# Attention pass of a four-layer graph network: each block of edges is summed by one flat scan over feature-major rows in PSUM instead of a tree of row-by-row multiply-adds

## The reference

```python
h = (x @ W_node).reshape(n, H, HD)                   # H = 4 heads of HD = 16
attn = a_src_node[src] + a_dst_node[dst] + edge_attr @ W_edge
attn = jnp.where(attn >= 0, attn, NEG_SLOPE * attn)
attn_max = jnp.zeros((n, H), attn.dtype).at[dst].max(attn)
attn = jnp.exp(attn - attn_max[dst])
attn_sum = jnp.zeros((n, H), attn.dtype).at[dst].add(attn)
attn = attn / (attn_sum[dst] + EPS_SOFTMAX)
msg = h[src] * attn[:, :, None]
out = jnp.zeros((n, H, HD), h.dtype).at[dst].add(msg).reshape(n, OUT_DIM)
y = out + h.reshape(n, OUT_DIM)                      # then a layernorm with gamma and beta
```

## Time and profile before

| what | value |
| --- | --- |
| time, median of 3 runs | 11177.78 us (11177.54 to 11199.18) |
| span of the profiled execution | 11181.7 us |
| profiled instructions | 57120 |
| DVE busy, whole span | 4736.9 us |
| ACT busy, whole span | 1142.1 us |
| POOL busy, whole span | 7106.9 us |
| attention pass, first gather to the end of the last | 8707.2 to 10967.1 us |

### The profile page before, as it was taken

The page is one execution under the profiler, slowest core; times in us unless marked ns, Lnnn a source line. Parts: engine busy times, 40 slices in busy tenths (PEclk is TensorE's granted clock), DMA queues, the critical chain, the costliest instruction groups (busy, mean ns, idle before and its releaser), DMA issues.

```text
span 11181.7 us, 57120 instructions
## 1 busy us (share of the span) xinstructions
PE 1801.6 (16%) x9285; PEld 1516.5 (14%) x9285; DVE 4736.9 (42%) x20005; ACT 1142.1 (10%) x2728; POOL 7106.9 (64%) x6884
## 2 busy tenths in 40 slices
PE   8744444444000400000000000000001000000000
PEld 7633333333000300000000000000000000000000
DVE  8855555555797422222221222222224344444446
ACT  0143434343000100000000000000000000000000
POOL 0566666666201377777776677777777776666766
PEclk7755555555555555555555555555555555555555
DMA  5144444444575111111111111111111222222221
GB/s 224 57 129 122 129 124 126 124 127 122 204 273 203 32 50 46 48 46 48 46 48 37 50 46 48 46 48 46 48 46 30 54 53 58 53 58 55 56 55 44
DMA packets 570444, 911.29 MB, mean 81 GB/s; under 512 B 333435, under 2 KB 348228, under 8 KB 544824
## 3 DMA queue, kind: packets, MB, share of 16 engines
q1 hardware_dynamic: 350264, 652.74, 17.3%
q0 software_dynamic: 219904, 255.88, 10.8%
HBM read 494.12 MB, written 414.02 MB: 81 GB/s over the span
## 4 chain that ended last, share of the span: by engine, by line
DVE 34%; issue 28%; another core or an unknown queue 17%; POOL 16%; PE 3%; DMA 1%; ACT 1%; DVEq 0%; SPq 0%; POOLq 0%; ACTq 0%
DVE arena_a L1495 16%; POOL arena_a L641 15%; DVE arena_b L1112 4%; DVE arena_a L1110 3%; DVE arena_b L1125 3%; DVE arena_a L1425 3%; POOL arena_a L610 2%; PE bank L811 2%; DVE arena_b L1056 1%; DVE arena_b L1093 1%; PE bank L916 1%; DVE arena_a L1625 0%; PE bank L890 0%; DMA arena_a<-in_a 0%
## 5 line engine op out<-in xcount | busy, mean ns | idle before, releaser
L641 POOL DMA_INDIRECT arena_a<-table_c,decay x3136 | 3284.6, 1047 | 1257.6 <-issue 1051.2
L1495 DVE SCALAR_TENSOR_TENSOR arena_a<-arena_a,same_dst 128x64 f32<-128x64 f32 x3134 | 891.5, 284 | 3449.5 <-DVE arena_a L1495 2713.2
L591 POOL DMA_INDIRECT by_src<-arena_b,idx_blk x1568 | 1570.8, 1002 | 885.8 <-issue 449.4
L641 POOL DMA_INDIRECT arena_a<-table_at,decay x1568 | 1556.8, 993 | 703.8 <-issue 468.4
L1110 DVE SCALAR_TENSOR_TENSOR arena_a<-arena_a,same_dst 128x64 f32<-128x64 f32 x1567 | 441.9, 282 | 711.1 <-remote 547.7
L864 PE MATMUL bank<-ident,chunk_end 128*64 128x128 f32 (+2 forms) x8 | 2.7, 442 | 4416.0 <-DVEq L973 4416.0
L864 PEld LDWEIGHTS bank<-ident,chunk_end 128*64 128x64 f32 (+2 forms) x8 | 1.4, 240 | 4416.6 <-DVEq L973 4416.6
L1112 DVE SCALAR_TENSOR_TENSOR arena_b<-arena_a,src_f,before 128x128 bf16<-128x128 f32 x1568 | 543.7, 347 | 37.4 <-issue 37.4
L850 PE MATMUL bank<-hrows 98*128 98x128 f32 x1568 | 404.0, 440 | 659.5 <-DVE arena_b L1125 331.9
L850 PE MATMUL bank<-hrows,arena_a 98*128 98x128 f32 x1568 | 403.3, 438 | 658.0 <-DVE arena_b L1125 347.4
L753 ACT ACTIVATE arena_b<-arena_a,decay 128x64 f32<-128x64 f32 x1568 | 394.2, 334 | 972.5 <-remote 610.2
(11 more groups left out here) (279 smaller groups left out, 4845.9 us busy)
## 6 DMA issues: line engine op xcount, KB each, us to landing
arena_a<-ids_rows SPq DMA_DIRECT2D x98, 1024.0 KB
states_src<-arena_a SPq DMA_DIRECT2D x98, 1024.0 KB
states_c<-arena_a SPq DMA_DIRECT2D x196, 512.0 KB
hrows<-by_src SPq DMA_DIRECT2D x98, 776.0 KB, 6.1
states_at<-arena_a SPq DMA_DIRECT2D x98, 576.0 KB
x_at_start<-arena_a SPq DMA_DIRECT2D x7, 7168.0 KB, 49.0
arena_a<-x_at_start SPq DMA_DIRECT2D x98, 512.0 KB
arena_a<-table_c,decay POOLq DMA_INDIRECT x3136
```

The costliest lines, as they stand in the source:

```text
L591: pool.indirect_dma_start(out=by_src, out_offset=AT(ap=idx_blk[r][:, k:k + 1], axis=0), in_=rows[r][:, k, :], in_offset=None)\
L641: pool.indirect_dma_start(out=gb[r][:, k * w:(k + 1) * w], out_offset=None, in_=table[g], in_offset=AT(ap=src_i[:, n * J + k:n * J + k + 1 ...
L1495: ins = v.scalar_tensor_tensor(out=st[h][:, k * D:(k + 1) * D], in0=old, scalar=same_dst[:, e:e + 1], in1=gb[r][:, k * D:(k + 1) * D], op0 ...
```

## The change

In the attention pass the tree of 33 operations goes. The rows to be summed now lie feature by feature: for each of the 68 columns, 17 slots of which slot 0 holds the carried sum and slots 1 to 16 the block's edges. That is 1156 elements per partition. A single scan `new = mask * old + in` over them makes all sums of the block; the mask is 0 in slot 0 of each column, so that one column does not run into the next. The input of the scan (`in0`) lies in PSUM, over three of its eight banks, and so do the exponentials (`p_ex`). DVE's weighing writes into `in0` directly, turned from edge-major to feature-major. ACT gets two new operations per block: `mask_spread` copies 16 mask values into all 68 columns, and `rows_back` turns the finished sums into the edge-major rows that SP stores, and raises `state`. POOL reuses a row buffer once the block in it is weighed (`weighed`). Before, it had to be summed. The score steps now stand in two groups, steps 0 to 2 ahead of the scan and 3 to 6 behind it. PE's two outputs move to other banks, the tables of products and their 14 operations go, and two memsets of the masks come in ahead of the first convolution. The convolutions keep their chain.

```diff
-                               ("ex", HEADS * (J + 1)), ("msk0", HEADS * (J + 1) + 1),
-                               ("msk1", HEADS * (J + 1) + 1), ("tmp", W3)])
+                               ("sums0", W3 * (J + 1)), ("sums1", W3 * (J + 1))])
...
+        by_feature = carve(arena_b[:, KN * W01 - 2 * W3 * (J + 1):], [(f"mask{h}", W3 * (J + 1)) for h in range(2)])
+        by_feature.update((name, late[name]) for name in ("sums0", "sums1"))
...
+        banks = ps("banks", [P, 8 * 512])
+        bank = [banks[:, n * 512:(n + 1) * 512] for n in range(8)]
+        by_feature.update((f"in{h}", banks[:, h * 3 * 512:(h + 1) * 3 * 512]) for h in range(2))
...
-        p_turned = [bank[1 + h][:, 0:J * E16] for h in range(2)]
-        p_score = [bank[3 + h][:, 0:J * HEADS] for h in range(2)]
+        p_turned = [bank[3 + h][:, 0:J * E16] for h in range(2)]
+        p_score = [bank[5 + h][:, 0:J * HEADS] for h in range(2)]
+        p_ex = bank[7][:, 0:HEADS * (J + 1)]
...
                 for n in range(NBLK):
-                    if n >= R:
+                    if n >= R and g == "at":
+                        pool.wait_ge(s("weighed"), n - R + 1)
+                    elif n >= R:
                         pool.wait_ge(s("state"), upto(g, "state") + n - R + 1)
...
+        def mask_spread(act, g, n):
+            w = W3 if g == "at" else D
+            if n >= 2:
+                act.wait_ge(s("summed"), upto(g, "summed") + n - 1)
+            act.activation(features(f"mask{n % 2}", w)[:, :, 1:J + 1], bf(same_dst[:, n * J:(n + 1) * J], w), ACT.Copy)\
+               .then_inc(s("mask_spread"), 1)
+        def rows_back(act, g, n):
+            w, row = (W3, W3S) if g == "at" else (D, D)
+            act.wait_ge(s("summed"), upto(g, "summed") + n + 1)
+            if n >= 2:
+                act.wait_ge(s(f"stored{n % 2}"), upto(g, f"stored{n % 2}") + 16 * (n // 2))
+            act.activation(st[n % 2][:, 0:J * row].rearrange("p (j f) -> p j f", f=row)[:, :, 0:w],
+                           features(f"sums{n % 2}", w)[:, :, 1:J + 1].rearrange("p f j -> p j f"), ACT.Copy)\
+               .then_inc(s("state"), 1)
...
                 act.wait_ge(s("at_args"), n + 1)
-                act.activation(late["ex"], late["df"], ACT.Exp).then_inc(s("at_exp"), 1)
-                g3 = gb[n % R].rearrange("p (j w) -> p j w", w=W3)
-                act.activation(by_head(g3)[:, :, :, HD], slots("df")[:, :, 1:J + 1].rearrange("p c j -> p j c"),
-                               ACT.Exp).then_inc(s("at_exp"), 1)
+                act.activation(p_ex, late["df"], ACT.Exp).then_inc(s("at_exp"), 1)
+                act.activation(weighed(n)[:, :, HD, 1:J + 1], slots("df")[:, :, 1:J + 1], ACT.Exp).then_inc(s("at_exp"), 1)
+                if n:
+                    rows_back(act, "at", n - 1)
+            rows_back(act, "at", NBLK - 1)
...
-            def sums_of(n, raw, carried, made, scored=None):
...
-                carried = chunk_end[:, 0:W3] if n == 0 else st[1 - h][:, (J - 1) * W3S:(J - 1) * W3S + W3]
                 if n:
-                    v.wait_ge(s("state"), upto("at", "state") + n)
-                v.tensor_tensor(late["tmp"].rearrange("p (c d) -> p c d", d=HS),
-                                carried.rearrange("p (c d) -> p c d", d=HS),
+                    v.wait_ge(s("summed"), upto("at", "summed") + n)
+                    carried = weighed(n - 1, "sums")[:, :, :, J]
+                else:
+                    carried = chunk_end[:, 0:W3].rearrange("p (c d) -> p c d", d=HS)
+                v.tensor_tensor(weighed(n)[:, :, :, 0], carried,
                                 slots("ex")[:, :, 0:1].to_broadcast([P, HEADS, HS]), ALU.mult)
-                hview = by_head(g3)[:, :, :, 0:HD]
-                v.tensor_tensor(hview, hview, ex_e.rearrange("p j (c o) -> p j c o", o=1)
+                v.tensor_tensor(weighed(n)[:, :, 0:HD, 1:J + 1].rearrange("p c d j -> p j c d"),
+                                by_head(g3)[:, :, :, 0:HD], ex_e.rearrange("p j (c o) -> p j c o", o=1)
                                 .to_broadcast([P, J, HEADS, HD]), ALU.mult).then_inc(s("weighed"), 1)
                 if ahead:
-                    score_step(n + 1, 0)
+                    for step in range(3):
+                        score_step(n + 1, step)
                 v.wait_ge(s("weighed"), n + 1)
-                sums_of(n, g3, late["tmp"], s3[:, :, 0:W3], n + 1 if ahead else None)
+                if n >= 2:
+                    v.wait_ge(s("state"), upto("at", "state") + n - 1)
+                v.tensor_tensor_scan(by_feature[f"sums{h}"], by_feature[f"mask{h}"],
+                                     by_feature["in0"][:, 0:W3 * (J + 1)], 0.0, ALU.mult, ALU.add).then_inc(s("summed"), 1)
+                if ahead:
+                    for step in range(3, 7):
+                        score_step(n + 1, step)
```

More of the change, by code:

```diff
@@ L55 @@
     "table_out": 16 * len(PARTS),
-    "onehots": 2 * NB, "onehots_used": 2 * NB, "flag": 1, "flagrow": 1, "chain": (J - 1) * NBLK,
+    "onehots": 2 * NB, "onehots_used": 2 * NB, "flag": 1, "flagrow": 1, "chain": (J - 1) * NBLK, "mask_spread": NBLK, "summed": NBLK,
 }
@@ L61 @@
                            CONVS))
+ORDER.update(dict.fromkeys(("mask_spread", "summed"), ("at",)))
 ORDER.update(dict.fromkeys(("onehots", "onehots_used"), ("dst", "src")))
@@ L347, in slots, with weighed @@
         def slots(name):
-            return late[name].rearrange("p (c j) -> p c j", j=J + 1)
+            return (p_ex if name == "ex" else late[name]).rearrange("p (c j) -> p c j", j=J + 1)
+        def weighed(n, name="in0"):
+            return features(name if name == "in0" else f"{name}{n % 2}", W3).rearrange("p (c d) j -> p c d j", d=HS)
         def rows_of(dram_ap, w):
@@ L357, in scattered, with features @@
             return s(f"scattered{n % R}"), n // R * (16 * J)
+        def features(name, w):
+            return by_feature[name][:, 0:w * (J + 1)].rearrange("p (f j) -> p f j", j=J + 1)
         def blk(i, h):
@@ L677, in dense_act @@
                 turned_act(act, g, p, i)
+        def mask_spread(act, g, n):
[12 more added lines that the diff above has]
+               .then_inc(s("state"), 1)
         def attention_act(act):
-            def mask_of(n):
-                act.activation(msk[n % 2][:, 0:HEADS * (J + 1)].rearrange("p (c j) -> p c j", j=J + 1)[:, :, 1:J + 1],
-                               bf(same_dst[:, n * J:(n + 1) * J], HEADS), ACT.Copy).then_inc(s("at_mask"), 1)
             def edges_turned(n):
@@ L691, in attention_act @@
             act.wait_ge(s("at_begun"), 1)
-            mask_of(0)
+            mask_spread(act, "at", 0)
             edges_turned(0)
@@ L1521, in conv_nodes @@
                 link(v.tensor_tensor(rows3, rows3, per_node(dinv, p, D), ALU.mult))
-            for span, product in run.items():
-                uppers = same_dst[:, :].rearrange("p (m two k) -> p m two k", two=2, k=span)[:, :, 1, :]
-                to = product.rearrange("p n (m k) -> p (n m) k", k=span)
-                link(v.tensor_copy(to, uppers))
-                for k in range(1, span):
-                    link(v.tensor_tensor(to[:, :, k], to[:, :, k], to[:, :, k - 1], ALU.mult))
+            for h in range(2):
+                link(v.memset(by_feature[f"mask{h}"], 0.0))
             conv("c1")
@@ L1565, in _ @@
             link(v.memset(late["mx"], 0.0))
-            for h in range(2):
-                link(v.memset(msk[h], 0.0))
             tell("at_begun")
@@ L1595, in score_step @@
                     v.wait_ge(s("score"), n * 5 + 3)
-                    v.wait_ge(s("at_mask"), n + 1)
-                    v.tensor_tensor_scan(late["fw"], msk[h][:, 0:slot_count], late["lk"], 0.0, ALU.mult, ALU.max)\
+                    v.wait_ge(s("mask_spread"), upto("at", "mask_spread") + n + 1)
+                    v.tensor_tensor_scan(late["fw"], by_feature[f"mask{h}"][:, 0:slot_count], late["lk"], 0.0, ALU.mult, ALU.max)\
                         .then_inc(s("score"), 1)
@@ L1600, in score_step @@
                     v.wait_ge(s("score"), n * 5 + 4)
-                    v.tensor_tensor_scan(late["mx"][:, ::-1], msk[h][:, 1:slot_count + 1][:, ::-1],
+                    v.tensor_tensor_scan(late["mx"][:, ::-1], by_feature[f"mask{h}"][:, 1:slot_count + 1][:, ::-1],
                                          late["fw"][:, ::-1], 0.0, ALU.mult, ALU.max).then_inc(s("score"), 1)
```

55 lines of the change are left out of this document (1 added, 54 removed).

## The result

The changed kernel takes 11108.16 us (median of 4 runs, 11103.21 to 11112.4), against 11185.37 us for the kernel before (median of 4 runs, 11177.54 to 11199.18). The ratio is 0.9926, with a 95% interval of 0.9912 to 0.994: faster by 0.7%. A second set, 5 runs against 9 on one chip, gives 0.9928 (0.9915 to 0.9942). The direction was forecast. The size was not: 290 us were expected, and 77 came.

The account below looks back on a forecast made before the run. POOL's gathers, delayed by a late DVE, were taken as the bound. Gathers 1950.6 plus 9.2 plus 15 make 1975 us instead of 2259.9, minus 285, with the tail minus 290: 10888 us, range 10868 to 10990.

Parts of the forecast that it names:

- The floor of POOL: Attention pass: a gather takes 0.944 us plus 0.30 before the next, so sixteen need at least 19.9 us per block.
- POOL's waits: Attention pass: POOL's waits for DVE's tree or a missing releaser go once buffers are free after weighing, minus 235.4 us.
- Count, not length: Attention pass: while POOL gathers, DVE gets one instruction per 1.3 to 1.4 us, so 43 need 57 us, 11 need 14.7.
- Stretch: Attention pass: DVE lengthens gathers by 76.6 us; 9.2 from four scans stay, 15 us are left for the rest.
- Prices: Attention blocks: scan 2.61 us, weighing 1.22, mask and copy of rows about 1.10 each, all hidden behind POOL's 19.9.
- the tail: Start of the last attention gather to first copy after the pass: 12.3 us instead of 17.0, 4.7 less.
- B: Rival, attention pass: DVE's instructions still come too slowly, fifteen at 1.40 us, 21.0 us per block; 10980 us, chance 0.15.
- D: Rival, attention pass: slow DVE instructions plus scan and weighing not overlapping, 24.8 us per block; slower, 11343 us, chance 0.05.
- E: Rival, attention pass: POOL's pauses have another cause than a late DVE and stay; nothing happens, 11178 us, chance 0.05.
- C: Rival, attention pass: scan and weighing hold gathers despite PSUM input, 2.3 us per block, 225 us; 11113 us, chance 0.05.

## Why the prediction was wrong, step by step

- **The floor of POOL, "sixteen of them make 19.9 us, the least that POOL needs for a block".** This is the step that failed. 19.98 us holds up to the eleventh block, then 22.40 (22.43 with the full kernel) is the least. The term "1568 x (0.944 + 0.30) = 1950.6" should have been that of the gathers alone, 2173.6 us, which has the four scans at its start in it. From 2260.3 that leaves 87 us to be had, and the change took 81. With 2173.6 in the place of 1975 the sum would have given some 11086 us, where 11108 was measured. The trace of before held the figure: both convolutions end in blocks of 22.40 us. In the first one, 9 blocks from the second on and 10 later are (length, POOL's busy time):

```profile
3870.20:4050.10 179.90, 136.02 (x144) 0.50 0.20 50
5167.40:5391.40 224.00, 169.72 (x161) 0.50 0.18 47
```

  I read that as DVE's chain, whose instructions come 1.40 us apart; it was POOL's, since with three DVE instructions per block in place of the chain these passes keep their length.
- **POOL's waits, -235.4 us.** They went, all of them. The price was wrong: a pause of POOL is given back as fast gathers (16.2 us for 16.2 in the run with one pause). By that run, the pauses of the kernel before had kept its gathers fast, so the limit did not show in this pass: its quickest blocks take 19.96 to 20.1 us from its start to its end.
- **Count, not length.** Right in kind: 43 instructions without length rebuild the old pass. As a fixed 1.33 us per instruction it is wrong, as 19 instructions show. The rows of before could have told: 4149 DVE instructions in 2259.9 us are one per 0.54 us, and 43 at 1.33 would need 57 us of a block of 23.06. Behind this: "Runtime: NRT & Kernel Launch" of the Trainium skill, section "Instruction fetch mechanics", has fetching mostly hidden. One-element copies 1.40 us apart are not bound by their work. In the pass with 43 instructions per block the queue that carries instructions moved 53 blocks of 8192 bytes, in 0.3 to 0.8 us each. That is few and short beside some 450 steps of 1.40 us, so a slow transfer of these blocks does not explain them; whether fetching is behind it in another way no run here shows.
- **Stretch, 15 us between 0 and 67.** The four scans are as before (longest gather 3357 ns). The rest of the 126 us of stretch (1606.7 - 1568 x 0.944) is the limit of 1.40 us, no hold by DVE: early blocks take 19.98 us with DVE's work and 19.97 without it. So the right size of the 15 us was nothing.
- **Prices.** Scan 2553 ns (2.61 forecast), weighing 1220 (1.22), mask 1110 (1.10): right. The copy of rows took 2107 ns, not 1.10 us. It has as many elements as the mask, so elements alone didn't fix the price. It is hidden but for the tail, 13.0 us against 12.3 forecast, 4.0 less than before instead of 4.7.
- **B and D** fell: no wait for `weighed`, DVE waits for rows at every block. **E** fell with POOL's pauses.
- **C, 11113 us,** is near the time by luck, for a reason that is wrong. The limit is there with no DVE at all, and a gather beside the large scan is not held (all 288 records of a gather beside one lie between 0.940 and 0.953 us), as the timeline of a late block shows:

```profile
9637.69 2.55 DVE L1595 TENSOR_TENSOR_SCAN arena_a<-arena_b,banks 128x1156 f32<-128x1156 f32 x1
9638.64 0.94 POOL L653 DMA_INDIRECT arena_a<-table_at,decay  x1 [0.30 <-issue]
```

  Here the rule of "SBUF — State Buffer" (the Trainium skill), section "Who interferes with whom", holds for a 2.55 us instruction with one input in SBUF and one in PSUM.

In the profiled executions, the pass up to the start of its last gather took 80.5 us less and the tail 4.0 less. 5.6 us were lost ahead of the pass: 8.6 by the start of the first convolution, some 6 of them in the pass over edges ordered by `src`, and 3.0 came back behind it. 4.6 were lost behind the tail: 3.3 ahead of the node gathers, where some of DVE's few instructions now start 1.2 us behind the one before, and 1.3 behind them. The change does not edit the instructions of either place, and nothing was tried on them. Together this is the span's -74.3.

What stays open: why the indirect form is held to one per 1.40 us over the long run; why DVE gets few instructions beside it; and why in the full kernel the delay falls on two gathers of a block and not on all. No run has the weighing alone shortened; the gathers without it keep the limit.

## What to carry to other kernels

Before you price a wait of the bounding engine at its full length, look for the longest unbroken stretch of that engine anywhere in the trace, in other passes too, and take its late pace for the floor: the median of one instruction between pauses need not be a rate that can be kept. Time the bare stream of the bounding instructions early; here one run of the gathers alone gives 2173.6 us and bounds at 87 us what any change can gain in this pass while it leaves these gathers as they are. And where the sum rests on "it would run at X if nobody waited", ask whether the waiting is what lets it run at X.

## What the runs showed of the hardware

- After a rest, or after a stretch at 1.43 us each, indirect gathers from POOL run at 1.25 us each for some 180 to 220, then at 1.40 us (22.40 us per 16). Rows per gather (64 or 128), bytes per row (16 or 272), a second POOL instruction each, and all other engines change nothing of the late pace. The starts of the passes show 26 to 30 us saved up at most, 27 of them after rests of 47 and of 160 us alike, and a pause of 16.2 us was given back one for one.
- Plain DMAs from POOL of as many rows, lying one behind the other, keep 0.53 us each with no such turn.
- Beside gathers, DVE's instructions of one element come as far as 1.40 us apart; with 19 per block the pass is 8 us longer than with 11, with 43 it is 108 us longer (2187.4 and 2287.2 against 2179.3).
- Gathers beside a scan of 1156 elements with one input in SBUF and one in PSUM took 0.940 to 0.953 us; beside a scan of 1568 with both inputs in SBUF one took 3.36 us.
- An ACT copy of 1088 elements took 1110 ns with one operand spread from 16 values, and 2107 ns when it turned feature-major sums into rows.
